# Sums on GpSimd moved behind the first maximum of a unit, four residual buffers, and another order of the tail

## The reference

```python
x = x + tanh(g_xattn[0]) * xattn(layernorm(x), ctx, Wq, Wk, Wv, Wo, q_norm_w, k_norm_w)
x = x + tanh(g_ffn[0]) * ffn(layernorm(x), router_w, router_b, A, Bm)

# xattn: 32 query heads, 8 key heads, head size 128
kv = concatenate([context, latents], axis=1)          # 461 rows
q, k, v = latents @ Wq, kv @ Wk, kv @ Wv              # q and k get an RMS norm per head
probs = softmax(q k^T / sqrt(128)); out = (probs v) @ Wo

# ffn: 8 experts of rank 16, the best two are used
logits = flat @ router_w.T + router_b; probs = softmax(logits)
topv, topi = top_k(probs, 2); gates = topv / sum(topv)
out = einsum(hw, Bm) * 0.5     # hw = (flat A^T) times the gate of its expert
```

## Time and profile before

| | us |
|---|---|
| median of 3 runs | 1715.18 (1713.99 to 1717.83) |
| the profiled execution | 1715.65 |
| its span | 1713.8 |
| PE busy | 1665.8 (97%) |
| DVE busy | 1239.6 (72%) |
| ACT busy | 865.1 (50%) |
| POOL busy | 873.9 (51%) |

### The profile page before, as it was taken

The page is one execution under the profiler, slowest core; times in us unless marked ns, Lnnn a source line. Parts: engine busy times, 40 slices in busy tenths (PEclk is TensorE's granted clock), DMA queues, the critical chain, the costliest instruction groups (busy, mean ns, idle before and its releaser), DMA issues.

```text
span 1713.8 us, 26112 instructions
## 1 busy us (share of the span) xinstructions
PE 1665.8 (97%) x9120; PEld 1475.3 (86%) x9120; DVE 1239.6 (72%) x2078; ACT 865.1 (50%) x1647; POOL 873.9 (51%) x668
## 2 busy tenths in 40 slices
PE   7999999999999999999999999999999999999996
PEld 6788888678888869899999999999999889999994
DVE  7788776677777742777777777777776876557767
ACT  5445554454444432555666565665555666443321
POOL 1454444134443320766767667788786445543320
PEclk9999999999999999999999999999999999999998
DMA  5667778636666564456555554666756557676632
GB/s 196 161 181 233 235 210 241 183 108 186 162 184 154 140 239 150 138 159 191 188 156 187 182 179 160 213 217 216 232 181 215 170 205 267 212 275 229 241 116 68
DMA packets 238502, 323.86 MB, mean 189 GB/s; under 512 B 53300, under 2 KB 193396, under 8 KB 233380
## 3 DMA queue, kind: packets, MB, share of 16 engines
q1 hardware_dynamic: 237796, 315.65, 59.8%
q10 hardware_dynamic: 576, 6.55, 0.9%
HBM read 212.18 MB, written 109.97 MB: 188 GB/s over the span
## 4 chain that ended last, share of the span: by engine, by line
PE 70%; DVE 18%; issue 4%; ACT 4%; DMA 2%; POOL 0%; DVEq 0%; SPq 0%; ACTq 0%; POOLq 0%
PE bank L973 21%; PE bank L975 20%; PE bank L974 20%; DVE mx L1923 4%; PE bank L1111 3%; DVE wq_lo L1805 3%; DVE q_lo L1897 3%; PE bank L1078 2%; DVE pT_lo L1917 2%; DMA kT_d<-kst 1%; PE bank L1007 1%; ACT pr L1539 1%; DVE q_raw L1875 1%; DVE nm L1929 1%; DVE wo_lo L1943 1%
## 5 line engine op out<-in xcount | busy, mean ns | idle before, releaser
L901 POOL TENSOR_SCALAR pr<-pr,rr 100x461 f32<-100x461 f32 x256 | 370.2, 1454 | 231.6 <-DVE rr L1938 231.6
L973 PE MATMUL bank<-w_hi,a_hi 128*128 128x512 f32 (+1 forms) x856 | 340.8, 398 | 11.7 <-DVE a_lo L1713 8.6
L975 PE MATMUL bank<-w_hi,a_lo 128*128 128x512 f32 (+1 forms) x856 | 334.8, 391 | 0.0
L974 PE MATMUL bank<-w_lo,a_hi 128*128 128x512 f32 (+1 forms) x856 | 334.3, 390 | 0.0
L1539 ACT ACTIVATE pr<-bank,nm,rq 100x461 f32<-100x461 f32 x256 | 188.8, 737 | 187.6 <-DVE nm L1929 186.2
L855 POOL TENSOR_TENSOR msk<-ssk,epst 128x4 f32<-128x4 f32 (+1 forms) x60 | 23.5, 391 | 348.5 <-DVE ssk L1744 348.5
L973 PEld LDWEIGHTS bank<-w_hi,a_hi 128*128 128x128 f32 (+1 forms) x856 | 157.8, 184 | 48.8 <-issue 9.7
L1923 DVE TENSOR_REDUCE mx<-bank 100x1 f32<-100x461 f32 x256 | 160.6, 627 | 48.7 <-PE bank L975 47.2
L975 PEld LDWEIGHTS bank<-w_hi,a_lo 128*128 128x128 f32 (+1 forms) x856 | 157.5, 184 | 38.0
L973 PE MATMUL bank<-xT_hi,wq_hi 128*128 128x400 f32 x512 | 188.9, 369 | 0.5 <-issue 0.5
L974 PEld LDWEIGHTS bank<-w_lo,a_hi 128*128 128x128 f32 (+1 forms) x856 | 158.0, 185 | 34.8
(11 more groups left out here) (154 smaller groups left out, 3635.1 us busy)
## 6 DMA issues: line engine op xcount, KB each, us to landing
kT_d<-kst SPq DMA_DIRECT2D x56, 512.0 KB, 5.7
v_d<-vst SPq DMA_DIRECT2D x56, 512.0 KB
kT<-kT_d SPq DMA_DIRECT2D x64, 361.0 KB, 4.5
kvr<-ctxT SPq DMA_DIRECT2D x44, 512.0 KB, 6.2
wq_raw<-Wq SPq DMA_DIRECT2D x32, 512.0 KB, 5.8
tb<-Wo SPq DMA_DIRECT2D x16, 1024.0 KB, 8.3
wt_d<-tb SPq DMA_DIRECT2D x16, 1024.0 KB, 8.0
wo_raw<-wt_d SPq DMA_DIRECT2D x16, 1024.0 KB, 7.4
```

The costliest lines, as they stand in the source:

```text
L901: pool.tensor_scalar(pr[0:NQ, u % 2, i], pr[0:NQ, u % 2, i], rr[0:NQ, i:i + 1], None, ALU.mult).then_inc(p_done, 1)
L973: pe.matmul(o, lh, rh, start=start, stop=False, skip_group_check=more)
L974: pe.matmul(o, lh, rl, start=False, stop=False, skip_group_check=more)
L975: return pe.matmul(o, ll, rh, start=False, stop=stop, skip_group_check=more)
```

## The change

There are three parts.

1. Sums on POOL. The first 16 weight sums (four steps) stand ahead of the first power of the mean squares, with their loads and stores in SP's loop over `AHEAD`; the other 48 stand one in each of units 0 to 47, behind a wait for the unit's first `nm` and ahead of its four scales. The early sums of head outputs are spread over units 8 to 52 (`S3_TIMES`). The power (`unit_rms`) stands behind the scales of the unit before instead of ahead of those of its own. SP issues a step's store and the next load one behind the other.
2. Four buffers of residual rows instead of two; all four first loads are issued together.
3. The tail. y of batches 4 to 7 is made by ACT (`Identity` with a scale and a bias), for which POOL makes two more small values. `low_rank` of batch 3 stands ahead of the last head product, its `up` ahead of the third `turn_out`, and the last `turn_y` ahead of the second `up`.

The core of the diff (the names of the new semaphores and some order in `next_res` and `store` are left out):

```diff
-WT_AT = {}
-for _n in range(4 * WT_STEPS):
-    WT_AT.setdefault(max(-1, (_n - 4) * 6 // 7), []).append(_n)
-WT_DONE = {n: next(u for u in WT_AT if 4 * n + 3 in WT_AT[u]) for n in range(WT_STEPS)}
-
-S3_AT = 34
+WT_FIRST = 4
+WT_DONE = [4 * (n - WT_FIRST) + 3 for n in range(WT_STEPS)]
+WT_LAST = WT_DONE[-1]
 S3_STEPS = GQ * TB
+S3_TIMES = sorted([(u, 1) for u in range(B, WT_LAST + 6, TB)] + [(WT_LAST + 1 + n, 0) for n in range(4)])[:S3_STEPS]
...
-        xr = at("xr", RAW, [P, 2, D])
+        xr = (at("xr0", RAW, [P, D]), at("xr1", RAW + 4 * KB, [P, D]), at("xr2", AOP + 10496, [P, D]),
+              at("xr3", TMP + 24 * KB, [P, D]))
...
             for n in range(AHEAD):
                 load_heads(n)
-                if n == AHEAD - 2:
+                if n == 0:
                     load_t(0)
                     load_t(1)
+                if n in (5, 6, 7, 8):
+                    store_t(n - 5)
+                    load_t(n - 3)
...
-                for n in range(WT_STEPS):
+                for n in range(WT_FIRST, WT_STEPS):
                     if u == WT_DONE[n] + 1:
                         store_t(n)
-                    if u == WT_DONE[n] + 2 and n + 2 < WT_STEPS:
-                        load_t(n + 2)
+                        if n + 2 < WT_STEPS:
+                            load_t(n + 2)
...
+            for i in range(4 * WT_FIRST):
+                weight_sum(i)
             unit_rms(0)
-            for i in WT_AT[-1]:
-                weight_sum(i)
             for u in range(UNITS):
-                if u % TB == TB - 1 and u + 1 < UNITS:
-                    unit_rms(u + 1)
+
+                if u <= WT_LAST:
+                    pool.wait_ge(nm_done, 4 * u + 1)
+                    weight_sum(4 * WT_FIRST + u)
+                if (u, 0) in S3_AT:
+                    pool.wait_ge(nm_done, 4 * u + 1)
+                    early_sum(S3_AT[u, 0])
                 for i in range(R):
                     scale(u, i)
-                for i in WT_AT.get(u, ()):
-                    weight_sum(i)
-                if 0 <= u - S3_AT - 1 < S3_STEPS:
-                    early_sum(u - S3_AT - 1)
+                if (u, 1) in S3_AT:
+                    early_sum(S3_AT[u, 1])
+                if u % TB == TB - 2 and u + 2 < UNITS:
+                    unit_rms(u + 2)
...
+                if t >= TB:
+                    pool.tensor_scalar(mv2[0:NQ, t, 2:3], mv[0:NQ, t, 0:1], -1.0, 0.0, ALU.mult, ALU.add).then_inc(mean_done, 1)
+                    pool.wait_ge(mean_done, t - TB + 1)
+                    pool.wait_ge(rs2_done, t + 1)
+                    pool.tensor_tensor(mv2[0:NQ, t, 3:4], mv2[0:NQ, t, 2:3], mv2[0:NQ, t, 1:2], ALU.mult).then_inc(scaled_done, 1)
...
                 for i in range(2):
                     chunk_head(TAIL0 + n // 2, n % 2 * 2 + i)
+                    if (n, i) == (4 * GQ - 1, 0):
+                        low_rank(TB - 1)
...
-            for do, t in ((turn_out, a), (turn_out, b), (turn_h, a - 1), (turn_out, c), (turn_y, a), (up, a - 1), (low_rank, a),
-                          (turn_out, d),
-                          (turn_y, b), (low_rank, b), (turn_h, a), (turn_y, c), (up, a), (low_rank, c), (turn_h, b), (up, b),
-                          (turn_y, d), (low_rank, d), (turn_h, c), (up, c), (turn_h, d), (up, d)):
+            for do, t in ((turn_out, a), (turn_out, b), (turn_h, a - 1), (up, a - 1), (turn_out, c), (turn_y, a), (low_rank, a),
+                          (turn_out, d), (turn_y, b), (low_rank, b), (turn_h, a), (turn_y, c), (up, a), (low_rank, c),
+                          (turn_h, b), (turn_y, d), (up, b), (low_rank, d), (turn_h, c), (up, c), (turn_h, d), (up, d)):
...
+            def norm(t):
+
+                act.wait_ge(scaled_done, t - TB + 1)
+                act.wait_ge(t2_done, t - 1)
+                act.activation(y[0:NQ, t % 2], x1[0:NQ, t % 4], ACT.Identity, bias=mv2[0:NQ, t, 3:4],
+                               scale=mv2[0:NQ, t, 1:2]).then_inc(y_done, 1)
...
-            exps2(TB - 1)
-            turned_h(TB - 1)
...
-            for do, t in ((turned_y, a), (exps2, a), (turned_y, b), (turned_h, a), (turned_y, c), (exps2, b),
-                          (turned_h, b), (turned_y, d), (exps2, c), (turned_h, c), (exps2, d), (turned_h, d)):
+            for do, t in ((exps2, a - 1), (turned_h, a - 1), (norm, a), (turned_y, a), (norm, b), (exps2, a), (turned_y, b),
+                          (norm, c), (turned_h, a), (turned_y, c), (exps2, b), (norm, d), (turned_h, b), (exps2, c),
+                          (turned_y, d), (turned_h, c), (exps2, d), (turned_h, d)):
...
+            route_top(TB - 1)
             accumulators(P3)
...
-            for do, t in ((route_top, a - 1), (residual, a), (route_gates, a - 1), (norm, a), (residual, b), (final, a - 1),
-                          (residual, c), (norm, b), (route, a),
-                          (norm, c), (residual, d), (route, b), (final, a), (norm, d), (route, c), (final, b), (route, d),
-                          (final, c), (final, d)):
+            for do, t in ((route_gates, a - 1), (residual, a), (residual, b), (final, a - 1), (residual, c), (route, a),
+                          (residual, d), (route, b), (final, a), (route, c), (final, b), (route, d), (final, c), (final, d)):
```

More of the change, by code:

```diff
@@ L150 @@
 WT_STEPS = GQ * R
[L151 to L157 removed]
+WT_FIRST = 4
+WT_DONE = [4 * (n - WT_FIRST) + 3 for n in range(WT_STEPS)]
+WT_LAST = WT_DONE[-1]
+S3_STEPS = GQ * TB
+S3_TIMES = sorted([(u, 1) for u in range(B, WT_LAST + 6, TB)] + [(WT_LAST + 1 + n, 0) for n in range(4)])[:S3_STEPS]
+S3_AT = {t: n for n, t in enumerate(S3_TIMES)}
+S3_LOAD = {}
+S3_STORE = {}
+for _n, (_u, _i) in enumerate(S3_TIMES):
+    S3_LOAD.setdefault(_u - 1, []).append(_n)
+    S3_STORE.setdefault(_u + 1, []).append(_n)
 UPPER = (P5, P4)
@@ L406, in build @@
         ffn_in = sem("ffn_in")
-        xr_in = [sem("xr_in0"), sem("xr_in1")]
+        xr_in = [sem(f"xr_in{i}") for i in range(4)]
         t1_done = sem("t1_done")
@@ L785, in _ @@
                     sp.dma_start(bm[:], BmT).then_inc(ffn_in, 16)
-                    load_res(0)
-                    load_res(1)
+                    for t in range(4):
+                        load_res(t)
             def next_res(t):
                 sp.wait_ge(x1_done, 2 * t + 2)
-                load_res(t + 2)
-            next_res(0)
+                load_res(t + 4)
             load_chunk(FIRST_OF[P3])
             load_chunk(FIRST_OF[P3] + 1)
-            next_res(1)
+            next_res(0)
             load_chunk(FIRST_OF[P3] + 2)
             store(0)
+            next_res(1)
             load_chunk(FIRST_OF[P3] + 3)
+            store(1)
             next_res(2)
-            store(1)
             store(2)
+            next_res(3)
             for t in range(TB - 1, B):
-                if t + 2 < B:
-                    sp.wait_ge(x1_done, 2 * t + 2)
-                    load_res(t + 2)
-                if t >= TB:
-                    store(t - 1)
-            store(B - 1)
+                store(t)
             sp.wait_ge(x2_stored[0], 16 * B // 2)
```

21 lines of the change are left out of this document (12 added, 9 removed).

## The result

The changed kernel takes **1728.8 us** (median of 4 runs, 1726.13 to 1730.86) against 1715.7 for the kernel before beside it (1713.99 to 1717.83). The ratio is 1.0075, 95% interval 1.0056 to 1.0094: slower, outside the predicted range of 1705 to 1720. The profiled execution took 1727.97, its span 1726.2: 12.3 us more than the profiled execution before.

A forecast was written before the change was run, and what follows sets the result against it. The prediction took PE to bound the attention stage and DVE to set the end of the tail. Start +17, steady part -14.5, tail -5 and residual buffers 0 gave -2.5: forecast 1713.0 us, range 1705 to 1720.

The forecast's parts named there:

- The moved sums, steady part: Attention units 2 to 51: sums behind the first nm free q_lo and wq_lo, even units fall to PE's floor; -14.5 us.
- the wait in SP's queue: Attention stage: a load waiting for a store's landing holds up only store_attn and load_vv, for less than a unit; 0.
- The start: Query stage: sixteen sums with their stores and loads delay Wq and the first scales; +17 us at unit 2, bounds +10 and +21.
- rival C: Start costs 21 us, the clock low when PE resumes and again in unit 1, tail gives 3; 1719.5 us, chance 0.18.
- the prediction's six steps: Start: with the skill page's 4.4 us per 1 MB instead of 5.7, six transfers would make the stall about 6 us shorter.
- the two parallel accounts of the prediction: Start: Wq of head 5 lands 18.7 us later, holding ACT, DVE and PE; POOL's sums make the first scales 16.8 later.
- The tail: After the last head product: y moved to ACT and reordered work let DVE end earlier; -5 us, bounds -7 and -2.
- Residual buffers: Four residual buffers: their loads move ahead of three stores, no residual in the tail waits for a load; 0.
- D: Rival: in its new place the sum stretches nm and delays the scales, even units keep 11.8; 1724.5 us, chance 0.10.
- V would come late ... some tenths in 12 units: Attention stage: if the store took more than a unit, V would come late and values wait, some tenths in 12 units.

The follow-up runs named there:

- e1: Changed kernel with the load of the next four Wo blocks issued one unit after the store of sums: 1717.45 us, ratio 1.0005 to the kernel before.
- e9: Kernel of e6 with the twelve extra sums behind the scales of odd units instead of even ones: 1699.23 us, ratio 0.9903 to the kernel before.
- e2: Kernel before with only the moves on POOL; start, SP queue, tail and residual buffers as before, some units with two sums: 1708.76 us, ratio 0.9951.
- e4: Changed kernel with the query stage's four store and load pairs queued behind the Wq load of head 5: 1721.39 us, ratio 1.0040 to the kernel before.
- e7: Kernel of e6 with eight sums at the start instead of four, none in units 0 to 2, eleven extra in even units: 1696.51 us, ratio 0.9893.
- e8: Changed kernel with four stores of sums cut to one partition of 128, the rest filled by copies of Wo in the stage ahead: 1733.26 us, ratio 1.0107.
- e3: Kernel before with only the new tail (part 3 of the change): 1711.75 us, ratio 0.9976 to the kernel before.
- e6: Changed kernel with e1's later load, four sums ahead of the first power, one in each of units 0 to 47, twelve more in even units: 1694.95 us, ratio 0.9874.
- e10: Kernel before with only the four residual buffers (part 2 of the change): 1716.65 us, ratio 1.0004 to the kernel before.

## Why the prediction was wrong

**The moved sums, steady part: right in its mechanism, wrong in one sentence.** q_lo and wq_lo no longer meet a sum at the end of odd units, even units last 11.34, and where nothing else is in the way the 50 units take 568.20 (e1): 14.7 less, forecast 14.5. e9 shows the parity, e2 that the gap holds one sum and not two. The step that failed is on SP's queue: "Queued behind that wait are store_attn and load_vv, which wait for the end of the unit anyway; a store of 5.7, or 8.4 behind another MB, is less than a unit. Nothing taken." So the wait in SP's queue was put at nothing, and it cost 9.7 us. It failed in three places. The size was short: in the kernel before the 15 stores of this kind from 710 to 1300 land after 8.1 in the median, which its list of DMA issues has:

```profile
wt_d<-tb SPq DMA_DIRECT2D x15, 1024.0 KB, 8.1
```

So the 8.4 was the usual case and not the bad one, and in the changed kernel the ten loads of this stage went out 8.4 to 9.8 behind their stores.

Then "less than a unit" was measured from the unit's start, where the store goes out 3.3 us into it (1169.19 - 1165.92; 2.6 in most such units), so 9.8 more leads into the next unit. And I looked at two items behind the wait and not at the third, the keys of the unit after, which are the most urgent of all: they went out 4.6 us into the unit instead of 1.3 (e1), with the waiting 1 MB now ahead of them. Cost in the profile: 9.7 us, of which 2.27 and the low clock behind it (unit 42, 3.1 longer) are the largest. e1 shows the cause: with the load behind the keys again, all of it is gone.

**The start: right in kind, 3 us short.** Forecast +17 at the start of unit 2, with bounds to +21; it was +19.6 by the stretch and +20.1 by the clock time. Up to the fourth load the working holds within a microsecond (third load forecast 681.8, issued 681.71; fourth 690.6, issued 691.33). Then three transfers are under way at once: the fourth load, Wq of head 5 and the third store landed after 9.4, 10.2 and 10.9 us:

```profile
tb<-Wo SPq DMA_DIRECT2D x1, 1024.0 KB, 9.4
```

I had given them 5.7, 7.1 and 7.1. My rule counted what stands ahead of a transfer (2.7 us for a MB) and left out what is issued behind it; that this is the whole of the difference is not shown. The first scales came at 712.6, forecast 707.0. Before that, at 704.7, PE resumes at the lower clock (0.51 until 710), as rival C said; unit 1 then ran at the full clock (11.42), which C had not. The Trainium skill, "DMA: Bandwidth & Descriptors", "Anatomy of one DMA", with its fixed 2.0 us would have led to a still shorter stall, with 4.4 for 1 MB (the prediction's six steps of 1.3 less are 7.8, not 6). The section measured DMAs issued by GpSimd, and these are issued by SP. The first store, alone, did land after 4.5 us; the stores and loads behind it took 6.4 to 10.9. e4 bears out the two parallel accounts of the prediction: neither Wq nor the sums alone set the end. e7 and e8 divide the price: eight sums at the start cost little more than four, the eight after them 21.9 with their stores and loads, and some 9 of these are the stores.

**The tail: right in its size, in part by luck.** Forecast -5, bounds -7 and -2; e3 gives -5.1 in the profile and -4.8 in the medians. DVE's busy time fell as worked out (29.85, by the sum 33.44 - 2.9 - 0.8 = 29.7), and PE waits 1.90 for the first y, forecast 2.2. But the sum gives the clock no term: the prediction expected the low one again, "as in this tail now". In the tails of all four kernels with the old order the granted clock is 0.50 in two stretches, some 10 us in all; in the eight with the new one it is so in a single stretch of 3 to 7 us. How much of the 5 us is the stretch that is gone, and which move took PE's stop of 3.60 away, is not separated. The changed kernel's own execution has -2.9. Its clock was 0.50 for the whole of 1696 to 1702, e3 for half as long, from 1679.5 to 1682.5. Of the eight kernels the three with the long stretch (this one, e6, e8) take 412.9 to 414.2 from unit 52 on, the other five 410.4 to 413.4.

**Residual buffers: right**, 0 (e10).

**The rivals.** C's start (+21) was nearly right, and D's time (1724.5) came nearest, but the reason is one that none of the rivals had. I had a sentence close to the true mechanism, "V would come late ... some tenths in 12 units", with the wrong operand and too low a price (nine units cost 9.1), and gave it no chance. With 568.2 for the steady part the same sum gives 19.6 - 14.7 - 5.1 = -0.2, and e1, which is that kernel, measured 1.0005, at 1717.45 inside the predicted range. So the term put at nothing is what led out of the range; the start, 3 us short, would not have done it alone.

## What to carry to other kernels

When a wait is put into an in-order DMA queue, go through the queue to the most urgent transfer behind it, not to the next one, and take the awaited transfer's duration from the stretch where it will run, with its neighbours. Work moved ahead of a stage has to be priced in round trips (store, landing, load, landing) and not in busy time alone: here eight sums at the start cost little more than four (1.7 us), and eight more, with a store and a load to land on the way, 21.9. A good part and two bad ones can hide in one number: the parts of this change put together without the early round trips and the store-load wait are 1.3% faster than before, where the whole was 0.75% slower.

## What the runs showed of the hardware

A wait of 2.27 us of PE was followed by 6.7 us at a granted clock of 0.51, the lower of its two levels (1.2 GHz), and made the next unit 3.1 longer. Behind the waits of 1.21 and 0.54 us at the ends of units 29 and 37 the granted clock stays at 1.00.

q_lo before a scale of pr alone took 0.90; in front of a head sum on POOL, at the end of unit 20 of the changed kernel, it took 1.34:

```profile
944.92 1.34 DVE L1924 TENSOR_TENSOR q_lo<-q_raw,q_hi 128x400 fp32r<-128x400 f32 x1 [0.27 <-ACT q_hi L1540]
```

The head sum follows POOL's scale at 946.15, only 0.11 before q_lo ends. The weight sum of the earlier trace rows likewise begins only 0.20 before q_lo ends that took 1.59. Spans on POOL are rough, so how long the two really overlapped stays open; it cost PE nothing in unit 20.

The 0.90 that the prediction took for an undisturbed q_lo isn't the shortest. Later in the changed kernel q_lo takes 0.57 while two scales of pr run on POOL (DVE, then POOL):

```profile
1388.20 0.57 DVE L1924 TENSOR_TENSOR q_lo<-q_raw,q_hi 128x400 fp32r<-128x400 f32 x1 [0.27 <-ACT q_hi L1540]
...
1387.08 3.56 POOL L910 TENSOR_SCALAR pr<-pr,rr 100x461 f32<-100x461 f32 x2 [5.25 <-DVE rr L1965]
```

So neither 0.57 nor 0.90 shows that the one shuts out the other for a whole instruction, but 0.90 has a lengthening of 0.33 in it whose cause no run here shows.

In the query stage eight sums beside DVE's copies and wq_lo took 11.44 us, 1.43 each, and 12.43 in e4, while four in a row took 5.16 in both, 1.29 each.

The first load of keys for attention, behind a keys-and-values stage of the same instructions in twelve kernels, went out between 658.2 and 661.3 us; in a comparison of single profiles that is as much as many an edit is worth, so stretches were measured from there.
